# Centring and gamma of every second batch on ScalarE and GpSimd, and b1 added by one matmul with one-hot weights

## The reference

```python
w1, w2 = W1[lang], W2[lang]                      # 512x128, 128x512 per batch
h = relu(einsum('bsh,bha->bsa', x, w1) + b1[lang])
adapted = einsum('bsa,bah->bsh', h, w2) + b2[lang]
y = x + adapted
mean, var = mean(y), mean((y - mean)**2)         # over the 512 columns
out = x + (y - mean) * rsqrt(var + 1e-5) * gamma[lang] + beta[lang]
```

## Time and profile before

| what | value |
|---|---|
| median of 3 runs | 325.21 us (325.19 to 325.84) |
| span of the profiled execution | 323.8 us |
| its TensorE | 301.9 us busy, 93% |
| its VectorE | 307.6 us busy, 95% |
| its ScalarE | 230.4 us busy, 71% |
| its GpSimd | 185.7 us busy, 57% |
| granted TensorE clock, mean | 0.969 |
| granted TensorE clock in the last of 40 slices | 0.5 |

### The profile page before, as it was taken

The page is one execution under the profiler, slowest core; times in us unless marked ns, Lnnn a source line. Parts: engine busy times, 40 slices in busy tenths (PEclk is TensorE's granted clock), DMA queues, the critical chain, the costliest instruction groups (busy, mean ns, idle before and its releaser), DMA issues. The chain is left out here.

```text
span 323.8 us, 8068 instructions
## 1 busy us (share of the span) xinstructions
PE 301.9 (93%) x2200; PEld 272.8 (84%) x2200; DVE 307.6 (95%) x679; ACT 230.4 (71%) x541; POOL 185.7 (57%) x217
## 2 busy tenths in 40 slices
PE   1659999999999999999999999999999999999962
PEld 1239899999999999999999999999999999999941
DVE  5687999999999999999999999999999999999996
ACT  3956677777777777877778777787777877778752
POOL 2960755556655566555665556655566555665553
PEclk9877999999999999999999999999999999999995
DMA  5999988766766667676776676766667666433324
GB/s 160 302 356 428 379 291 273 236 228 231 257 232 227 228 229 263 223 233 226 230 256 232 228 231 227 261 236 221 231 225 262 221 234 232 160 132 134 130 108 152
DMA packets 41711, 75.69 MB, mean 234 GB/s; under 512 B 2253, under 2 KB 7404, under 8 KB 41542
## 3 DMA queue, kind: packets, MB, share of 16 engines
q1 hardware_dynamic: 41571, 75.04, 68.5%
q10 hardware_dynamic: 99, 0.14, 0.1%
HBM read 41.62 MB, written 33.55 MB: 232 GB/s over the span
## 5 line engine op out<-in xcount | busy, mean ns | idle before, releaser
L295 POOL TENSOR_TENSOR x_io<-x_io,beta_all 128x512 f32<-128x512 f32 x128 | 161.2, 1280 | 0.0
L401 PE MATMUL ps_h<-w_all,x_T 128*128 x1024 | 137.0, 284 | 0.0
L401 PEld LDWEIGHTS ps_h<-w_all,x_T 128*128 128x128 f32 x1024 | 126.1, 194 | 1.6
L345 ACT ACTIVATE cut<-ps_y,row_sum 128x512 bf16<-128x512 f32 x128 | 88.0, 688 | 24.0 <-PE ps_y L428 24.0
L572 DVE SCALAR_TENSOR_TENSOR x_io<-ps_y,rstd,x_io 128x512 f32<-128x512 f32 x128 | 90.2, 747 | 2.5 <-DVE rstd L564 0.3
L559 DVE SCALAR_TENSOR_TENSOR ps_y<-ps_y,mean,gamma_all 128x512 f32<-128x512 f32 x128 | 90.8, 754 | 0.8 <-ACT cut L345 0.6
L292 POOL TENSOR_TENSOR mean<-row_sum,over_h 128x2 f32<-128x2 f32 x64 | 12.9, 201 | 125.6 <-DVE ps_y L540 113.6
L540 DVE SCALAR_TENSOR_TENSOR ps_y<-x_io,b_all 128x512 f32<-128x512 f32 x124 | 83.1, 713 | 0.0
L393 PE MATMUL ps_T<-identity,x_io 128*128 128x128 f32 x512 | 68.2, 277 | 10.0 <-DMA x_io<-in_x 10.0
L393 PEld LDWEIGHTS ps_T<-identity,x_io 128*128 128x128 f32 x512 | 61.1, 143 | 19.1 <-issue 10.4
L322 ACT COPY x_T<-ps_T 128x1024 f32<-128x1024 f32 x64 | 63.7, 995 | 8.2 <-PE ps_T L393 8.2
(11 more groups left out here) (60 smaller groups left out, 173.6 us busy)
## 6 DMA issues: line engine op xcount, KB each, us to landing
x_io<-in_x SPq DMA_DIRECT2D x64, 512.0 KB, 4.4
out<-x_io SPq DMA_DIRECT2D x63, 512.0 KB, 3.0
x_io<-in_L_cond_W SPq DMA_DIRECT2D x5, 512.0 KB, 7.2
w_all<-in_L_cond_W SPq DMA_DIRECT2D x5, 512.0 KB, 8.9
b_all<-in_L_cond_b SPq DMA_DIRECT2D x1, 2560.0 KB, 15.7
out<-x_io SPq DMA_DIRECT2D x2, 256.0 KB, 2.0
x_io<-in_L_cond_gamma SPq DMA_DIRECT2D x1, 60.0 KB
x_io<-in_L_cond_beta ACTq DMA_DIRECT2D x1, 60.0 KB
```

The costliest lines, as they stand in the source:

```text
L295: nc.gpsimd.tensor_tensor(x_slot(t), x_slot(t), of_lang(beta_all, langs[b]), ALU.add)\
L345: nc.scalar.activation(squares[:, t % 2, :], ps_y[t % Y_BANKS][:, :], ACT.Square, scale=-float(H), bias=stat(row_sum, t), accum_out=stat(s ...
L401: last = nc.tensor.matmul(part, x_T[:, t % 4, c, :], w1_all[:, bass.ds(lang, 1), c, :].rearrange("p o a -> p (o a)"), start=False, stop=(c ...
```

## The change

For each pair the second batch (b = 1) leaves VectorE's scaling. ScalarE takes the mean off while it copies the bank into a new SBUF tile `centred` (two buffers), after `square_pair`. GpSimd multiplies `centred` by gamma in place (`gain`), between its two additions of beta of the next pair. VectorE finishes that batch from `centred` one pair later (`finish_second(n - 1)` after `scale_first(n)`). The bank of a second batch can be seeded again when it is squared and centred. GpSimd now stores the negative mean.

b1 of a pair is added by one matmul with 256 columns for both batches: `b1_pair` holds b1's parts in rows 0 to 29 for the first batch and 32 to 61 for the second, zero elsewhere, and the weights are one column of `is_lang`, repeated 128 times. `is_lang` is made at the start from the ids, which are now loaded to 64 partitions. `pick_row` gets a second set of rows, by three more affine_selects. `cut` has two tiles of 512 instead of three, and H_PAIRS is 4.

```diff
-H_PAIRS = 6
+H_PAIRS = 4
@@ GpSimd
+            def mean_of_pair(n):
                 pool.wait_ge(seeded, 2 * n + 2)
-                pool.wait_ge(x_turned, 2 * n + 2)
-                nc.gpsimd.tensor_tensor(stats(mean, n), stats(row_sum, n), over_h[:, 0:2], ALU.mult).then_inc(mean_ready, 1)
...
+            def add_beta(t, lang):
+                pool.wait_ge(x_turned, t + 1)
+                nc.gpsimd.tensor_tensor(x_slot(t), x_slot(t), of_lang(beta_all, lang), ALU.add).then_inc(x_beta_ready, 1)
+
+            def gain(n, lang):
+                pool.wait_ge(centred_ready, n + 1)
+                nc.gpsimd.tensor_tensor(centred[:, n % 2, :], centred[:, n % 2, :], of_lang(gamma_all, lang), ALU.mult)\
+                    .then_inc(gained, 1)
...
             for n in range(PAIRS):
-                add_beta(n)
+                langs[n] = langs_of(pool, n)
+                mean_of_pair(n)
+                add_beta(2 * n, langs[n][0])
+                if n > 0:
+                    gain(n - 1, langs[n - 1][1])
+                add_beta(2 * n + 1, langs[n][1])
+            gain(PAIRS - 1, langs[PAIRS - 1][1])
@@ ScalarE
+            def centre(n):
+                t = 2 * n + 1
+                act.wait_ge(adapted, t + 1)
+                act.wait_ge(mean_ready, n + 1)
+                if n >= 2:
+                    act.wait_ge(out_ready, 2 * (n - 2) + 2)
+                nc.scalar.activation(centred[:, n % 2, :], ps_y[t % Y_BANKS][:, :], ACT.Identity,
+                                     bias=stat(neg_mean, t)).then_inc(centred_ready, 1)
...
             for p in range(FIRST, PAIRS):
                 square_pair(p - FIRST)
+                centre(p - FIRST)
                 step(p)
@@ TensorE
-                nc.tensor.matmul(part, of_lang(pick, lang), b1_parts[:, :], start=True, stop=False)
+                nc.tensor.matmul(pair_of(ps_h), is_lang[:, p:p + 1].broadcast_to([128, S]),
+                                 b1_pair[:, :, :].rearrange("p b a -> p (b a)"), start=True, stop=True)
@@ VectorE, seed_pair
-                    if t >= Y_BANKS:
+                    if t >= Y_BANKS and b == 0:
                         dve.wait_ge(out_ready, t - Y_BANKS + 1)
+                    if t >= Y_BANKS and b == 1:
+                        dve.wait_ge(centred_ready, n - 1)
+                        dve.wait_ge(squared, t - Y_BANKS + 1)
@@ VectorE, finish
+            def finish_second(n):
+                t = 2 * n + 1
+                dve.wait_ge(rstd_ready, n + 1)
+                dve.wait_ge(gained, n + 1)
+                dve.wait_ge(x_beta_ready, t + 1)
+                nc.vector.scalar_tensor_tensor(x_slot(t), centred[:, n % 2, :], stat(rstd, t), x_slot(t),
+                                               ALU.mult, ALU.add).then_inc(out_ready, 1)
...
             def norm_and_seed(n, p):
-                scale_pair(n, langs[n])
+                scale_first(n, langs[n][0])
                 if n + 2 < PAIRS:
                     langs[n + 2] = langs_of(dve, n + 2)
+                if n > 0:
+                    finish_second(n - 1)
                 invert_pair(n)
-                finish_pair(n)
+                finish_first(n)
```

More of the change, by code:

```diff
@@ L41, in build @@
     by_dve = [n for n in range(2 * L) if n not in by_act]
-    assert FIRST + 2 <= H_PAIRS
+    assert FIRST + 1 <= H_PAIRS
+    HALF_ROWS = 32
+    PAIR_ROWS = 2 * HALF_ROWS
+    assert 3 * L <= HALF_ROWS
     with ExitStack() as ctx:
@@ L70, in build @@
         b1_rows = sb("b1_rows", [3 * L, A], F32)
-        b1_parts = sb("b1_parts", [128, A], BF16)
+        b1_parts = sb("b1_parts", [3 * L, A], BF16)
+        b1_pair = sb("b1_pair", [128, 2, A], BF16)
+        count_row = sb("count_row", [128, L], F32)
+        lang_of_row = sb("lang_of_row", [128, 1], F32)
+        is_lang = sb("is_lang", [128, PAIRS], BF16)
+        centred = sb("centred", [128, 2, H], F32)
         later_part = sb("later_part", [128, 2], F32)
@@ L89, in build @@
         row_sum = sb("row_sum", [128, SLOTS], F32)
-        mean = sb("mean", [128, SLOTS], F32)
+        neg_mean = sb("neg_mean", [128, SLOTS], F32)
         sq_sum = sb("sq_sum", [128, SLOTS], F32)
@@ L116, in build @@
         set_ready = sem("set_ready")
-        over_h_ready = sem("over_h_ready")
+        neg_over_h_ready = sem("neg_over_h_ready")
+        count_row_ready = sem("count_row_ready")
+        lang_of_row_ready = sem("lang_of_row_ready")
+        is_lang_ready = sem("is_lang_ready")
+        b1_pair_ready = sem("b1_pair_ready")
+        centred_ready = sem("centred_ready")
+        gained = sem("gained")
         later_part_ready = sem("later_part_ready")
@@ L209, in load_x @@
                 sp.dma_start(x_pair_slots(p), x_pairs[:, p, :, :]).then_inc(x_loaded[p % X_PAIRS], 16)
[L211 removed]
+            sp.dma_start(ids_raw[:, :], ids.partition_broadcast(PAIR_ROWS)).then_inc(s_ids, 16)
             sp.dma_start(x_io[0:3 * L, 2 * ROWS_PAIR, :],
@@ L258, in _ @@
             pool.wait_ge(set_ready, 4)
-            for g in range(3):
+            for g in range(6):
                 nc.gpsimd.affine_select(out=pick_row[:, :], in_=pick_row[:, :], compare_op=ALU.not_equal, fill=1.0,
-                                        base=-L * g, pattern=[[-1, L]], channel_multiplier=1).then_inc(pick_step, 1)
+                                        base=-L * (g % 3) - HALF_ROWS * (g // 3), pattern=[[-1, L]],
+                                        channel_multiplier=1).then_inc(pick_step, 1)
                 pool.wait_ge(pick_step, g + 1)
+            nc.gpsimd.iota(count_row[:, :], [[1, L]], base=0, channel_multiplier=0,
+                           allow_small_or_imprecise_dtypes=True).then_inc(count_row_ready, 1)
             nc.gpsimd.affine_select(out=later_part[:, :], in_=later_part[:, :], compare_op=ALU.is_ge, fill=0.0,
@@ L286, in _ @@
             cut_in_three(b2_rows[:, :], b2_cut[:, 1, :], parts[0:3 * L, 2 * H:3 * H], 4, b2_parts_ready)
-            def add_beta(n):
-                langs = langs_of(pool, n)
+            def mean_of_pair(n):
                 pool.wait_ge(seeded, 2 * n + 2)
-                pool.wait_ge(x_turned, 2 * n + 2)
-                nc.gpsimd.tensor_tensor(stats(mean, n), stats(row_sum, n), over_h[:, 0:2], ALU.mult).then_inc(mean_ready, 1)
[L293 to L296, removed]
+                nc.gpsimd.tensor_tensor(stats(neg_mean, n), stats(row_sum, n), neg_over_h[:, 0:2], ALU.mult)\
+                    .then_inc(mean_ready, 1)
+            def add_beta(t, lang):
[5 more added lines that the diff above has]
+                    .then_inc(gained, 1)
             pool.wait_ge(ids_ready, 1)
-            pool.wait_ge(over_h_ready, 2)
+            pool.wait_ge(neg_over_h_ready, 1)
             pool.wait_ge(spread_act, len(by_act))
             pool.wait_ge(spread_dve, len(by_dve))
+            langs = {}
             for n in range(PAIRS):
-                add_beta(n)
+                langs[n] = langs_of(pool, n)
[5 more added lines that the diff above has]
+            gain(PAIRS - 1, langs[PAIRS - 1][1])
         @block.scalar
@@ L380, in _ @@
                 square_pair(p - FIRST)
+                centre(p - FIRST)
                 step(p)
             square_pair(PAIRS - FIRST)
+            centre(PAIRS - FIRST)
             high_h(PAIRS - 1)
@@ L385, in _ @@
                 square_pair(n)
+                centre(n)
         @block.tensor
@@ L395, in turn_x, with first_products @@
                 last.then_inc(x_turned, 1)
-            def first_product(t, lang):
-                part = pair_of(ps_h)[:, (t % 2) * A:(t % 2 + 1) * A]
-                nc.tensor.matmul(part, of_lang(pick, lang), b1_parts[:, :], start=True, stop=False)
[L400 to L405, removed]
+            def first_products(p, langs):
+                nc.tensor.matmul(pair_of(ps_h), is_lang[:, p:p + 1].broadcast_to([128, S]),
+                                 b1_pair[:, :, :].rearrange("p b a -> p (b a)"), start=True, stop=True)
+                for b in range(2):
+                    t = 2 * p + b
+                    for c in range(C):
+                        last = nc.tensor.matmul(pair_of(ps_h)[:, b * A:(b + 1) * A], x_T[:, t % 4, c, :],
+                                                w1_all[:, bass.ds(langs[b], 1), c, :].rearrange("p o a -> p (o a)"),
+                                                start=False, stop=False, skip_group_check=True)
+                last.then_inc(h_summed, 1)
             def turn_h(p):
@@ L467, in _ @@
                     turn_h(p - 1)
-                for b in range(2):
-                    first_product(2 * p + b, langs[p][b])
+                first_products(p, langs[p])
                 if p < PAIRS - 1:
@@ L485, in _ @@
             nc.vector.memset(parts[:, :], 0.0).then_inc(parts_zero, 1)
-            nc.vector.memset(b1_parts[:, :], 0.0).then_inc(parts_zero, 1)
+            nc.vector.memset(b1_pair[:, :, :], 0.0).then_inc(parts_zero, 1)
```

(40 more changed lines are left out.)

21 lines of the change are left out of this document (10 added, 11 removed).

## The result

The changed kernel takes 400.7 us (400.48 to 400.91, 4 runs) against 325.2, a ratio of 1.231 (95% interval 1.229 to 1.233): 23% slower. The forecast was 398.

The account below looks back on a forecast made before the run. TensorE was taken as the bound at 4.49 us a pair, VectorE within 0.05. To the 323.8 us span came 71.4 (period), 0.2 and 0.5 (start), 0.9 (end); with 1.4 from span to median, 398, range 356 to 412.

Parts of the forecast that it names:

- The exclusion: VectorE instructions with two SBUF inputs and GpSimd's tensor_tensor shut each other out; VectorE holds 0.59 us, GpSimd 1.10.
- The hold of a product of 128x512: GpSimd's beta additions and gamma product each shut VectorE's two-SBUF-input instructions out for 1.10 us, three times a pair.
- rival 3: GpSimd and VectorE exclude each other for whole durations: 6.42 us a pair, 445 us in all; chance 0.09.
- The period: Mean of one pair to the next: 5.66 us against 4.49, +1.17 a pair, x 61 = +71.4 us.
- The end: After the last mean: the last finish waits for a last gamma product, ending at 6.4 instead of 5.54, +0.9 us.
- the distance from span to time: The median time of 325.2 us lies 1.4 over the span of 323.8; added to the forecast span of 396.8.
- The start: Before the steady part: ids on 64 partitions hold back DMAs, +0.2 us; the later first seed pair adds 0.5.
- `centre`: ScalarE's added 128x512 PSUM to SBUF pass: 0.65 us a pair, taken up by the 0.8 us wait at `copy_h`.
- The b1 saving: TensorE, one b1 matmul of 256 columns for two: 0.11 us a pair saved, step 4.38, lost in the longer period.
- Rival 1: No exclusion between VectorE and GpSimd for these instructions; TensorE stays the bound: 319.6 us; chance 0.07.
- Rival 2: GpSimd holds a shorter part, 0.77 us of 1.28, as a tensor_scalar suggested: 357 us; chance 0.10.
- Rival 4: TensorE's clock also falls, from a 1.3 us gap in each 5.66; near 590 us if all at 1.2 GHz; chance 0.04.

Follow-up runs that it names:

- the extra product: Kernel before the change, plus one GpSimd 128x512 product per pair of two tables into a spare tile nobody reads (H_PAIRS 5): 374.4 us against 326.0.
- b2 by matmul: Changed kernel with b2 put in the bank by bfloat16 matmul for every batch, so VectorE's seed has one SBUF input: 356.2 us.
- the dose in between: Changed kernel with GpSimd's gamma product on only 256 of the 512 columns of the second batches: 366.65 us.

## Why the prediction was right

**What bounds the kernel.** TensorE at 4.49 and VectorE within 0.05 of it: with only b1 changed the gain stopped at 4.43, where VectorE was put.

**The exclusion, from five instructions of the start**. Shown from both sides: more of it with nothing else changed (the extra product, 326.0 to 374.4), less of it with the work kept (b2 by matmul, 400.7 to 356.2), and the dose in between. The hold of a product of 128x512 was taken as 1.10 and measured 1.11 (first addition: 184.54 to 185.65), 1.14 (the extra product) and 1.15 (second addition); that of VectorE's instruction was taken as 0.59 and measured 186.23 - 185.65 = 0.58. The whole durations, rival 3, would have put the period at 6.42. The Trainium skill, "SBUF — State Buffer", section "SBUF: two separate sides", has the lock held for the whole instruction. Here the measurement decides: the last 0.13 to 0.18 us of an addition do not hold it.

**The period.** 5.66 forecast, 5.69 measured: from the mean of pair 2 at 42.14 to that of pair 63 at 389.41 there are 61 periods. The 0.03 a pair make 2.0 of the 2.7 us by which the forecast was low. The end adds 0.4 (the last finish ends 6.8 us after the last mean, not 6.4) and the distance from span to time, 1.7 instead of 1.4, adds 0.3. The start takes off 0.5: the mean of pair 2 comes at 42.14, 0.2 after that of the earlier trace rows instead of 0.7. The 0.5 that is left is the rounding of the forecast's own terms (71.4 for 71.6, 398 for 398.2) and 0.1 behind the last finish. So the total is a little better than its terms, which partly cancel; the period, which carries the forecast, is right by itself.

**The other terms.** `centre` takes 0.67 (0.65 taken) and is hidden by the wait at `copy_h`. The b1 saving was taken as 0.11 and is 0.13, just above the 0.06 to 0.12 given for it, and all of it lies in TensorE's wait.

**The rivals.** Rival 1 (no exclusion) fell with the period and with the run with the extra product. Rival 2 (a hold of 0.77) fell with 1.14; the tensor_scalar that did not delay L523 in the earlier trace rows is no measure for a tensor_tensor. Why it let L523 in, although it reads SBUF, stays open. Rival 4: the granted clock stayed 1.00 from 100 to 380 us with a gap of 1.15 us in each pair.

## What to carry over

Before work is moved to GpSimd, list VectorE's instructions that read two SBUF tensors and find when each engine's run: where they meet, GpSimd's microseconds are added to VectorE's, even if GpSimd looks half idle in the shares (57% here). The remedy is in the operands: let one input of VectorE come from PSUM, or let GpSimd only write. The first took 44 us off the changed kernel, and memsets beside the seeds cost nothing. And a sum of busy time hides this, because a shut-out instruction counts as busy: compare the mean duration of the same operation before and after.

## What was unexpected

A GpSimd power on 128x2 elements takes 0.70 us, a product of that size 0.20. Weights that are one column repeated 128 times load as fast as those of `pick`: 98 ns against 99, and the matmul follows at once. And GpSimd, with three waits on its own results, stood idle for 0.4 to 0.6 us before its next mean although nothing that the trace shows was missing.
